# A feed-forward stage's SiLU and channel maximum: one pass per group of four channel chunks, or one pass over all 32

## The chip, the cores and the metric

The kernel runs on all 8 cores of one Trainium2 chip. The batch of 16 sequences is dealt out two to a core, every core runs the same program on its own two, and no core talks to another. The metric is the device time of the slowest core in microseconds (us). The profile shown is one execution, read on core 5, which took longest in it.

## What is computed

The reference is a transformer layer: attention with its layer norms, then a quantized feed-forward stage (BitNet style) with a depthwise convolution in it. Cut to the part that the change touches:

```python
def bit_linear(x, w):            # act_quant: per token, scale 127 / max |x| over channels
    xq = act_quant(x)            # weight_quant: to -1, 0, 1 by mean |w|
    wq = weight_quant(w)
    return einsum('bsd,hd->bsh', xq, wq)
h = bit_linear(x, w1)                                # 1024 -> 4096 channels
h = depthwise_conv1d(h, conv_w, conv_b)              # 3 taps along the tokens
h = silu(h)
return bit_linear(h, w2)                             # 4096 -> 1024 channels
```

The second `bit_linear` needs, for each token, the largest |silu(h)| over all 4096 channels before it can quantize any of them. That maximum is what the changed lines compute.

## The kernel before

Each core handles its two sequences one after the other (`_seq`), with these stages in a row: layer norm and transposes, the three projections, attention, output projection and second layer norm, weight quantization (reloaded for the second sequence), the feed-forward stage (`_p5_ffn`), and a last layer norm with the output.

In `_p5_ffn` the loop runs over 16 token tiles of 128 tokens (NT = 16), so 32 tiles in all on a core. In a tile the 4096 hidden channels lie as 32 chunks (HC = 32) of 128 channels on the 128 partitions, tokens along the free dimension; `tcv` holds the tile's hidden activations, 32 chunks by 128 tokens, bf16. A tile goes like this:

- For each chunk TensorE runs 8 matmuls (L851) into one of two small PSUM tensors, `hps0` and `hps1`. It may not write one until VectorE has emptied the chunk two before (`hevac`).
- VectorE empties it with the two dequantization scales into `hgr` (L863), 130 columns wide, since the convolution wants a token on either side.
- After every fourth chunk (`c4 == 3`), VectorE runs the convolution of that group of four in six instructions (L888 to L898) into 512 columns of `tcv`.
- Still within the group, ScalarE applies SiLU to these 512 columns in place (L901). VectorE waits for it and takes the maximum of |value| over the group's four chunks for every token (L905, a strided read: for each of 128 tokens four values that lie 128 elements apart). From the second group on that goes into a scratch column block of `f12`, and a further instruction merges it into `gmax` (L912). There are 8 groups in a tile.
- After the eighth group TensorE transposes `gmax` (L914), VectorE reduces it over the partitions' 128 rows, works out the scale, and the scale is spread over the partitions (L917 to L935).
- Then for each of 8 blocks of 512 columns, GpSimd multiplies by the scale (L949), VectorE and GpSimd round by hand in five steps (L953 to L967), and TensorE runs 8 matmuls of 512 columns with the quantized weights `w2q` (L978). VectorE takes the tile's result out of PSUM (L989) and a DMA stores it (L993).

The order of the work is the order of the program text. `em.emit` appends to one stream per engine, and an engine runs its stream in order. Every VectorE instruction waits for the one before it (semaphore `dv`, through `emit`), and a wait with `None` means everything that engine had been given by then. So the instruction that waits for ScalarE at L905 holds back everything behind it on VectorE, the next group's L863 among it:

```python
em.emit("vector", lambda e, g_=g_: e.tensor_reduce(
    gmax[:] if g_ == 0 else f12[:, 0:128], ...),
    waits=[(ac, None)])
```

Of the kernel before, what the change touches and what calls it, by code (L numbers as in the profile page):

```python
# [9 lines left out]
AF = mybir.ActivationFunctionType  # L10
ALU = mybir.AluOpType
AX = mybir.AxisListType
# [10 lines left out]
HC = DH // 128  # L23
# [71 lines left out]
def rearr(t, spec, **kw):  # L95
    return t[:].rearrange(spec, **kw)
# [171 lines left out]
def _seq(ctx, s):  # L268
    nc = ctx["nc"]
    with (  # L270
        nc.sbuf_tensor(f"s{s}_xqfm", [128, DC * S], BF16) as xqfm,
        nc.sbuf_tensor(f"s{s}_ivfm", [128, S], F32) as ivfm,
    ):
        with nc.sbuf_tensor(f"s{s}_big32", [128, DC * S], BF16) as big32:
            with (
                nc.sbuf_tensor(f"s{s}_qpk", [128, DC * S], BF16) as qpk,
                nc.sbuf_tensor(f"s{s}_kpk", [128, DC * S], BF16) as kpk,
                nc.sbuf_tensor(f"s{s}_vsb", [128, NT * VW], BF16) as vsb,
            ):
                _p1_ln1(ctx, s, big32)  # L280
                _p2_qkv(ctx, s, big32, qpk, kpk, vsb, (xqfm, [0, DC * D]))
                with (
                    nc.sbuf_tensor(f"s{s}_pt", [128, 3 * S], BF16) as pt,
                    nc.sbuf_tensor(f"s{s}_oddh", [64, S], BF16) as oddh,
                    nc.sbuf_tensor(f"s{s}_qa", [65, 2 * S], BF16) as qa,
                    nc.sbuf_tensor(f"s{s}_ka", [65, 2 * S], BF16) as ka,
                    nc.sbuf_tensor(f"s{s}_mke", [64, 65], BF16) as mke,
                ):
                    ctx["ivb16"] = xqfm
                    ctx["absq"] = oddh  # L290
                    _p3_attn(ctx, s, qpk, kpk, vsb, big32, pt, ivfm, oddh,
                             qa, ka, mke)
            _p4_proj_ln(ctx, s, big32, xqfm, ivfm)
        with (
            nc.sbuf_tensor(f"s{s}_w1q", [128, DC * DH], BF16) as w1q,
            nc.sbuf_tensor(f"s{s}_w2q", [128, HC * D], BF16) as w2q,
        ):
            _p45_wquant(ctx, s, w1q, w2q)
            _p5_ffn(ctx, s, xqfm, ivfm, w1q, w2q)
# [504 lines left out]
def _p5_ffn(ctx, s, xqfm, ivfm, w1q, w2q):  # L804
    nc, dr, sb, em = ctx["nc"], ctx["dr"], ctx["sb"], ctx["em"]
    pe, dv, ac = ctx["pe"], ctx["dv"], ctx["ac"]
    sf, sws = ctx["sf"], ctx["sws"]
    fspill = []
    with (
# [25 lines left out]
        for i in range(NT):  # L835
# [3 lines left out]
            for cc in range(HC):  # L839
                idx = i * HC + cc  # L840
                g, c4 = cc // 4, cc % 4
                ps = hps[cc % 2]
                if idx >= 2:
                    w = [(dv, hevac[idx - 2])]
                else:
                    w = [(dv, None)]
                    if ctx.get("wq_rdy"):
                        w.append((sws, ctx["wq_rdy"]))
                for dc in range(DC):
                    em.emit("tensor", lambda e, ps=ps, cc=cc, dc=dc,  # L850
                            j0=j0, j1=j1, t0=t0: e.matmul(  # L851
                        ps[:, j0:j1],
                        w1q[:, dc * DH + cc * 128:dc * DH + cc * 128 + 128],
                        xqfm[:, dc * S + t0 + j0:dc * S + t0 + j1],
                        start=(dc == 0), stop=(dc == DC - 1)),
                        inc=pe if dc == DC - 1 else None,
                        waits=w if dc == 0 else [])
                gb = (g % 2) * 520
                hw = [(pe, None)]
                if len(convd) >= 2:  # L860
                    hw.append((dv, convd[-2]))
                em.emit("vector", lambda e, ps=ps, c4=c4, gb=gb, j0=j0, j1=j1,
                        t0=t0: e.scalar_tensor_tensor(  # L863
                    hgr[:, gb + c4 * 130 + j0:gb + c4 * 130 + j1],
                    ps[:, j0:j1], sb["iwcol"][:, 0:1],
                    ivfm[:, t0 + j0:t0 + j1], ALU.mult, ALU.mult),
                    waits=hw)
                if i == 0:
                    em.emit("vector", lambda e, c4=c4, gb=gb: e.memset(
                        hgr[:, gb + c4 * 130:gb + c4 * 130 + 1], 0.0))  # L870
                if i == NT - 1:
                    em.emit("vector", lambda e, c4=c4, gb=gb: e.memset(
                        hgr[:, gb + c4 * 130 + 129:gb + c4 * 130 + 130], 0.0))
                hevac.append(dv.n)
                if c4 == 3:
                    def hv(j, gb=gb):
                        return bass.AP(hgr, gb + j, [[1040, 128], [130, 4],
                                                     [1, 128]])
                    def wmap(j, g=g):
                        return bass.AP(sb["cw"], 3 * (4 * g) + j,  # L880
                                       [[3 * HC, 128], [3, 4], [0, 128]])
                    cbm = bass.AP(sb["cb"], 4 * g,
                                  [[HC, 128], [1, 4], [0, 128]])
                    out3 = bass.AP(tcv, g * 512, [[HC * 128, 128], [128, 4],
                                                  [1, 128]])
                    tm3 = bass.AP(tmpg, 0, [[512, 128], [128, 4], [1, 128]])
                    em.emit("vector", lambda e, hv=hv, wmap=wmap, out3=out3:
                            e.tensor_tensor(out3, hv(1), wmap(1), ALU.mult))  # L888
                    em.emit("vector", lambda e, cbm=cbm, out3=out3:
                            e.tensor_tensor(out3, out3, cbm, ALU.add))  # L890
                    em.emit("vector", lambda e, hv=hv, wmap=wmap, tm3=tm3:
                            e.tensor_tensor(tm3, hv(0), wmap(0), ALU.mult))
                    em.emit("vector", lambda e, out3=out3, tm3=tm3:
                            e.tensor_tensor(out3, out3, tm3, ALU.add))
                    em.emit("vector", lambda e, hv=hv, wmap=wmap, tm3=tm3:
                            e.tensor_tensor(tm3, hv(2), wmap(2), ALU.mult))
                    em.emit("vector", lambda e, out3=out3, tm3=tm3:
                            e.tensor_tensor(out3, out3, tm3, ALU.add))  # L898
                    convd.append(dv.n)
                    g_ = cc // 4  # L900
                    em.emit("scalar", lambda e, g_=g_: e.activation(  # L901
                        tcv[:, g_ * 512:(g_ + 1) * 512],
                        tcv[:, g_ * 512:(g_ + 1) * 512], AF.Silu),
                        waits=[(dv, None)])
                    em.emit("vector", lambda e, g_=g_: e.tensor_reduce(  # L905
                        gmax[:] if g_ == 0 else f12[:, 0:128],
                        bass.AP(tcv, g_ * 512, [[HC * 128, 128], [1, 128],
                                                [128, 4]]),
                        AX.X, ALU.max, apply_absolute_value=True),
                        waits=[(ac, None)])  # L910
                    if g_ > 0:
                        em.emit("vector", lambda e: e.tensor_max(  # L912
                            gmax[:], gmax[:], f12[:, 0:128]))
            em.emit("tensor", lambda e: e.transpose(  # L914
                tmps[:], gmax[:], sb["eye32"][:]), inc=pe,
                waits=[(dv, None), (dv, None)])
# [12 lines left out]
                waits=[(dv, None)])  # L929
# [6 lines left out]
                    waits=[(pe, None)])  # L936
# [6 lines left out]
            for g in range(8):  # L943
# [3 lines left out]
                if i >= 1 and g == 0:  # L947
# [6 lines left out]
                        waits=[(ctx["gc"], yg)])  # L954
# [8 lines left out]
                    waits=[(ctx["gc"], dg)])  # L963
# [7 lines left out]
                for cc4 in range(4):  # L971
                    cc = g * 4 + cc4
# [3 lines left out]
                    for nb in range(2):  # L976
# [7 lines left out]
                            waits=w2w if (nb == 0 and cc4 == 0) else [])  # L984
# [103 lines left out]
```

How the kernel before makes its waits and increments, by code:

```python
        def play(e, fn=fn, wl=wl, inc=inc, k=k):  # L72
            for h, v in wl:
                e.wait_ge(h, v)
            ins = fn(e)
            if inc is not None and ins is not None:
                ins.then_inc(inc.h, k)
# [82 lines left out]
        @blk.sync  # L160
        def _(sync):
            sync.wait_ge(sems["so0"].h, sems["so0"].n)
            sync.wait_ge(sems["so1"].h, sems["so1"].n)
```

## Time and profile before

| | us |
|---|---|
| two timed runs | 8022.25 and 8098.92, median 8060.58 |
| the profiled execution | 8044.94 |
| span of its slowest core (core 5), first to last instruction | 8043.3 |
| spans of the eight cores | 8003.8 to 8043.3 |
| first feed-forward stage in it (window used here) | 2050 to 3970 |
| second feed-forward stage (window used here) | 5900 to 7900 |

In the rows below PE is TensorE (PEld its weight loads), DVE is VectorE, ACT is ScalarE and POOL is GpSimd. A row of a group of instructions reads: line, engine, operation, output and inputs with shapes, count, then the busy time in us and the mean ns of one, then the idle time of the engine just before them in us and what ended it. A row of the timeline reads: start in us, length in us, engine, line, operation, count, and in brackets the idle time before it and its releaser. "PEclk" is TensorE's granted clock as a share of full speed.

### The profile page before, as it was taken

Reading aid. Unit: us, or ns where it says so; the run is one execution under the profiler, and the core shown is the slowest. Engines: PE = TensorE matmul, PEld = TensorE weight load, DVE = VectorE, ACT = ScalarE, POOL = GpSimd, SP = SyncE. Lnnn points to the kernel's source line nnn. Section 1 sums busy time; section 2 is a strip of 40 time slices with the busy share of each in tenths; the row PEclk is TensorE's granted clock in tenths of the full one; section 3 lists DMA queues with packets and bytes.
Section 4 is the critical chain, followed back from the end, with each engine's and each line's share of the span. In section 5 each row is a group of like instructions: output and inputs, shape, how many; then the busy total and the mean of one; then the engine's idle time right before and its main releaser. Section 6 shows DMA issues by size and latency. Waiting matters only on the chain. (4 is left out here: it accounts for less than half of the span.)

```text
span 8043.3 us, 59576 instructions; the slowest of 8 cores (8003.8 to 8043.3 us)
## 1 busy us (share of the span) xinstructions
PE 3718.8 (46%) x17510; PEld 1781.4 (22%) x17510; DVE 4463.2 (55%) x6308; ACT 1248.6 (16%) x1418; POOL 675.0 (8%) x630
## 2 busy tenths in 40 slices
PE   0688886220334343343416888862224334344341
PEld 0322222110222222222203222221112222222221
DVE  5334444557666666666653444436546666666665
ACT  0035554000000000000000465540000000000000
POOL 0000000000011111111110000000001111111111
PEclk9877887665666666666657877776666666666665
DMA  6200001114300000000042000011020000000004
GB/s 192 52 6 6 8 8 21 37 37 141 118 3 6 3 6 6 3 6 3 6 144 58 7 7 6 8 26 37 34 86 6 6 3 6 3 6 6 3 6 128
DMA packets 59132, 251.98 MB, mean 31 GB/s; under 512 B 6720, under 2 KB 6848, under 8 KB 55232
## 3 DMA queue, kind: packets, MB, share of 16 engines
q1 hardware_dynamic: 40992, 197.32, 7.7%
q0 software_dynamic: 17824, 50.86, 2.3%
q8 instruction: 147, 2.41, 0.1%
q14 instruction: 169, 1.38, 0.1%
HBM read 185.77 MB, written 67.11 MB: 31 GB/s over the span
## 5 line engine op out<-in xcount | busy, mean ns | idle before, releaser
L851 PE MATMUL s_hps<-s_xqfm,s_w1q 128*128 128x130 bf16 (+1 forms) x8192 | 864.1, 293 | 1665.2 <-DVE s_hgr L863 1232.4
L851 PEld LDWEIGHTS s_hps<-s_xqfm,s_w1q 128*128 128x128 bf16 x8192 | 775.9, 134 | 1759.3 <-issue 1737.1
L534 ACT ACTIVATE s_pt<-s_sc 128x1024 bf16<-128x1024 f32 x1024 | 1048.7, 1024 | 691.2 <-PE s_sc L521 620.1
L978 PE MATMUL s_fp<-s_w2q,s_gq 128*128 128x512 bf16 x2048 | 707.9, 508 | 716.6 <-DVE s_gq L967 716.6
L521 PE MATMUL s_sc<-s_qa,s_ka 65*128 65x512 bf16 x2048 | 753.8, 459 | 142.7 <-ACT s_pt L534 27.3
L901 ACT ACTIVATE s_tcv<-s_tcv 128x512 bf16<-128x512 bf16 x256 | 161.1, 629 | 3777.8 <-DVE s_tcv L898 3777.8
L547 PE MATMUL s_atps<-s_pt,s_vsb 128*65 128x512 bf16 x2048 | 668.6, 423 | 0.0
L961 DVE SCALAR_TENSOR_TENSOR s_f<-s_db,s_r 128x512 f32<-128x512 f32 x256 | 396.1, 1547 | 406.6 <-POOL s_db L958 406.6
L949 POOL TENSOR_TENSOR s_yb<-s_tcv,s_sgb 128x512 f32<-128x512 bf16 x256 | 296.1, 1157 | 3780.5 <-DVE s_sgb L935 3748.4
L863 DVE SCALAR_TENSOR_TENSOR s_hgr<-s_hps,iwcol,s_ivfm 128x130 bf16<-128x130 f32 (+1 forms) x1024 | 361.3, 353 | 437.0 <-PE s_hps L851 376.7
L978 PEld LDWEIGHTS s_fp<-s_w2q,s_gq 128*128 128x128 bf16 x2048 | 225.2, 118 | 1188.5 <-issue 1102.8
L556 DVE COPY s_ivfm<-s_atps 65x2048 f32<-65x2048 f32 x32 | 73.2, 2287 | 674.7 <-PE s_atps L547 674.7
L564 DVE RECIPROCAL s_ivfm<-s_ivfm 1x2048 f32<-1x2048 f32 x32 | 414.2, 12944 | 3.3
L958 POOL TENSOR_TENSOR s_db<-s_yb,s_r 128x512 f32<-128x512 f32 x256 | 323.1, 1262 | 614.6 <-DVE s_r L955 614.6
L905 DVE TENSOR_REDUCE s_f<-s_tcv 128x128 f32<-128x512 bf16 x224 | 227.2, 1014 | 213.9 <-ACT s_tcv L901 213.9
L521 PEld LDWEIGHTS s_sc<-s_qa,s_ka 65*128 65x128 bf16 x2048 | 163.8, 105 | 700.1 <-issue 687.6
L547 PEld LDWEIGHTS s_atps<-s_pt,s_vsb 128*65 128x65 bf16 x2048 | 252.3, 124 | 298.7 <-issue 126.3
L725 PE MATMUL s_trp<-eye16s,s_xqt 128*128 128x128 bf16 x256 | 32.4, 306 | 603.1 <-DVE s_xqt L262 603.1
L378 PE MATMUL s_qps<-s_big,s_xqfm 128*128 128x512 bf16 x1024 | 249.0, 412 | 39.2 <-DMA s_xqfm<-wq_t 39.2
L246 ACT ACTIVATE sdc<-st 128x1 f32<-128x1 f32 x128 | 26.0, 203 | 1160.0 <-DVE st L241 1159.9
L579 PE MATMUL s_sc<-s_ivfm,ones 1*64 1x512 f32 x256 | 169.5, 818 | 76.3 <-DVE s_xqfm L566 48.4
L676 PE MATMUL s_op<-s_wo,s_big 128*128 128x512 bf16 x512 | 174.3, 516 | 40.3 <-DMA s_wo<-wo_t 40.3
(123 smaller groups left out, 3723.1 us busy)
## 6 DMA issues: line engine op xcount, KB each, us to landing
s_xint<-x SPq DMA_DIRECT2D x64, 512.0 KB, 3.9
p0st<-w_t SPq DMA_DIRECT2D x8, 2048.0 KB, 8.9
p0st<-w_t SPq DMA_DIRECT2D x32, 512.0 KB, 3.3
x2scr<-s_x2t SPq DMA_DIRECT2D x32, 512.0 KB, 2.9
s_wst<-w_t SPq DMA_DIRECT2D x16, 1024.0 KB, 5.0
s_wst<-w_t SPq DMA_DIRECT2D x32, 512.0 KB, 3.2
fscr<-s_ft POOLq DMA_DIRECT2D x32, 512.0 KB, 3.0
s_frl<-fscr SPq DMA_DIRECT2D x32, 512.0 KB, 6.5
```

Of the source, the lines that this page charges most:

```text
L378: wo=wofs[wb]: e.matmul(ps[:, nb * 512:(nb + 1) * 512], wtens[:, wo + dc * D + oc * 128:wo + dc * D + oc * 128 + 128], xn1[:, dc * S + nb ...
L521: em.emit("tensor", lambda e, kt=kt, nb=nb, b=b, j=j: e.matmul(scp[j][:, nb * 512:(nb + 1) * 512], ka[:, b * S + kt * 128:b * S + kt * 128 ...
L534: em.emit("scalar", lambda e, p=p, j=j: e.activation(pt[:, p * S + j * Q:p * S + (j + 1) * Q], scp[j][:], AF.Exp), waits=w)
L547: em.emit("tensor", lambda e, kt=kt, nb=nb, h=h, p=p, j=j: e.matmul(atps[0:65, j * Q + nb * 512:j * Q + (nb + 1) * 512], vsb[:, kt * VW + ...
L564: em.emit("vector", lambda e: e.reciprocal(ivr[64:65, :], ivr[64:65, :]))
L851: j0=j0, j1=j1, t0=t0: e.matmul(ps[:, j0:j1], w1q[:, dc * DH + cc * 128:dc * DH + cc * 128 + 128], xqfm[:, dc * S + t0 + j0:dc * S + t0 + j1],
L863: t0=t0: e.scalar_tensor_tensor(hgr[:, gb + c4 * 130 + j0:gb + c4 * 130 + j1], ps[:, j0:j1], sb["iwcol"][:, 0:1], ivfm[:, t0 + j0:t0 + j1] ...
L905: em.emit("vector", lambda e, g_=g_: e.tensor_reduce(gmax[:] if g_ == 0 else f12[:, 0:128], bass.AP(tcv, g_ * 512, [[HC * 128, 128], [1, 128],
L949: em.emit("gpsimd", lambda e, ts=ts: e.tensor_tensor(rearr_ap3(yb), rearr_ap3(ts), sgv, ALU.mult), inc=ctx["gc"], waits=yw)
L958: em.emit("gpsimd", lambda e: e.tensor_sub(db2[:], yb[:], r02[:]), inc=ctx["gc"], waits=[(dv, r0d)])
L961: em.emit("vector", lambda e: e.scalar_tensor_tensor(f12[:], db2[:], 1.5, r02[:], ALU.is_gt, ALU.add), waits=[(ctx["gc"], dg)])
L978: gq4=gq4, cc4=cc4: e.matmul(ps[:, nb * 512:(nb + 1) * 512], gq4[:, cc4 * 128:(cc4 + 1) * 128], w2q[:, cc * D + nb * 512:cc * D + (nb + 1) ...
```

## The change

The SiLU and the maximum are taken out of the group's branch and out of the loop over chunks. They are issued once per tile, after the last chunk: one ScalarE instruction over all 4096 columns of `tcv`, in place, and one VectorE reduction that reads, for each of 128 tokens, 32 values 128 elements apart, straight into `gmax`. The merging instruction is gone. The reduction still waits for ScalarE, and the transpose behind it (now L905) still waits for the reduction.

```diff
                     convd.append(dv.n)
-                    g_ = cc // 4
-                    em.emit("scalar", lambda e, g_=g_: e.activation(
-                        tcv[:, g_ * 512:(g_ + 1) * 512],
-                        tcv[:, g_ * 512:(g_ + 1) * 512], AF.Silu),
-                        waits=[(dv, None)])
-                    em.emit("vector", lambda e, g_=g_: e.tensor_reduce(
-                        gmax[:] if g_ == 0 else f12[:, 0:128],
-                        bass.AP(tcv, g_ * 512, [[HC * 128, 128], [1, 128],
-                                                [128, 4]]),
-                        AX.X, ALU.max, apply_absolute_value=True),
-                        waits=[(ac, None)])
-                    if g_ > 0:
-                        em.emit("vector", lambda e: e.tensor_max(
-                            gmax[:], gmax[:], f12[:, 0:128]))
+            em.emit("scalar", lambda e: e.activation(tcv[:], tcv[:], AF.Silu),
+                    waits=[(dv, None)])
+            em.emit("vector", lambda e: e.tensor_reduce(
+                gmax[:], rearr(tcv, "p (c t) -> p t c", c=HC), AX.X, ALU.max,
+                apply_absolute_value=True), waits=[(ac, None)])
```

On VectorE, at the border between two groups in the middle of a tile, before (L863 is the emptying of the next group's four chunks, L888 its convolution's first instruction):

```order
L896 TENSOR_TENSOR s_tmpg<-s_hgr,cw_sb 128x512
L898 TENSOR_TENSOR s_tcv<-s_tcv,s_tmpg 128x512
L905 TENSOR_REDUCE s_f<-s_tcv 128x128
L912 TENSOR_TENSOR s_gmax<-s_gmax,s_f 128x128
L863 SCALAR_TENSOR_TENSOR s_hgr<-s_hps,iwcol,s_ivfm 128x130 x4
L888 TENSOR_TENSOR s_tcv<-s_hgr,cw_sb 128x512
```

The same border on VectorE after the change:

```order
L896 TENSOR_TENSOR s_tmpg<-s_hgr,cw_sb 128x512
L898 TENSOR_TENSOR s_tcv<-s_tcv,s_tmpg 128x512
L863 SCALAR_TENSOR_TENSOR s_hgr<-s_hps,iwcol,s_ivfm 128x130 x4
L888 TENSOR_TENSOR s_tcv<-s_hgr,cw_sb 128x512
L890 TENSOR_TENSOR s_tcv<-s_tcv,cb_sb 128x512
```

The reduction and the merge have left the border, and the emptying of the next chunks stands right behind the convolution.

On VectorE at the end of a tile, before (L917 reads the transposed `gmax`):

```order
L898 TENSOR_TENSOR s_tcv<-s_tcv,s_tmpg 128x512
L905 TENSOR_REDUCE s_f<-s_tcv 128x128
L912 TENSOR_TENSOR s_gmax<-s_gmax,s_f 128x128
L917 TENSOR_REDUCE sdc<-s_tmp 128x1
L919 TENSOR_SCALAR sdc<-sdc 128x1
```

The same place after the change, where lines behind the diff have moved up by nine:

```order
L898 TENSOR_TENSOR s_tcv<-s_tcv,s_tmpg 128x512
L902 TENSOR_REDUCE s_gmax<-s_tcv 128x128
L908 TENSOR_REDUCE sdc<-s_tmp 128x1
L910 TENSOR_SCALAR sdc<-sdc 128x1
L912 RECIPROCAL sdc<-sdc 128x1
```

One reduction (L902) now stands there in place of a reduction and a merge, and it is the only one of the tile.

On ScalarE one sequence's feed-forward stage holds, in the piece of the difference below, 128 instructions before and 16 after:

```order
-L901 ACTIVATE s_tcv<-s_tcv 128x512 x128
+L900 ACTIVATE s_tcv<-s_tcv 128x4096 x16
```

The work per element is the same; the number of instructions falls to an eighth. On TensorE and GpSimd no instruction is moved.

## Rows read from the trace of the kernel before

**Rows 1.** The page's first part: busy time of each engine over the span.

```profile
PE 3718.8 (46%) x17510; PEld 1781.4 (22%) x17510; DVE 4463.2 (55%) x6308; ACT 1248.6 (16%) x1418; POOL 675.0 (8%) x630
```

**Rows 2.** The page's fourth part, the chain that ended last, by engine.

```profile
DMA 1%; DVE 0%; issue 0%; ACT 0%; DVEq 0%; POOLq 0%; ACTq 0%; SPq 0%
```

**Rows 3.** Busy time of each engine in the two feed-forward stages.

```profile
core 5: us, PE busy (x) PEld busy (x) DVE busy (x) ACT busy (x) POOL busy (x), PEclk, DMA share, GB/s
2050.00:3970.00 1920.00, 766.20 (x4932) 487.44 (x4933) 1181.56 (x2084) 77.42 (x122) 299.27 (x255) 0.65 0.04 13
5900.00:7900.00 2000.00, 785.07 (x5120) 504.70 (x5120) 1227.33 (x2194) 81.82 (x129) 302.81 (x258) 0.65 0.02 6
```

**Rows 4.** Timeline of one group in the middle of a tile, 2582 to 2595 us.

```profile
2582.05 0.42 DVE L898 TENSOR_TENSOR s_tcv<-s_tcv,s_tmpg 128x512 bf16<-128x512 bf16 x1
2582.63 0.63 ACT L901 ACTIVATE s_tcv<-s_tcv 128x512 bf16<-128x512 bf16 x1 [8.60 <-DVE s_tcv L898]
2583.43 1.01 DVE L905 TENSOR_REDUCE s_f<-s_tcv 128x128 f32<-128x512 bf16 x1 [0.95 <-ACT s_tcv L901]
2584.55 0.29 DVE L912 TENSOR_TENSOR s_gmax<-s_gmax,s_f 128x128 f32<-128x128 f32 x1
2584.94 0.81 DVE L863 SCALAR_TENSOR_TENSOR s_hgr<-s_hps,iwcol,s_ivfm 128x130 bf16<-128x130 f32 x2
...
2585.44 3.62 PE L851 MATMUL s_hps<-s_xqfm,s_w1q 128*128 128x130 bf16 x32 [6.00 <-DVE s_hgr L863]
2586.64 0.35 DVE L863 SCALAR_TENSOR_TENSOR s_hgr<-s_hps,iwcol,s_ivfm 128x130 bf16<-128x130 f32 x1 [0.89 <-PE s_hps L851]
2587.51 0.35 DVE L863 SCALAR_TENSOR_TENSOR s_hgr<-s_hps,iwcol,s_ivfm 128x130 bf16<-128x130 f32 x1 [0.51 <-PE s_hps L851]
...
2594.56 0.81 DVE L863 SCALAR_TENSOR_TENSOR s_hgr<-s_hps,iwcol,s_ivfm 128x130 bf16<-128x130 f32 x2
```

**Rows 5.** Groups of instructions by line and shape: SiLU, maximum and merge.

```profile
L905 DVE TENSOR_REDUCE s_f<-s_tcv 128x128 f32<-128x512 bf16 x224 | 227.2, 1014 | 213.9 <-ACT s_tcv L901 213.9
...
L901 ACT ACTIVATE s_tcv<-s_tcv 128x512 bf16<-128x512 bf16 x256 | 161.1, 629 | 3777.8 <-DVE s_tcv L898 3777.8
...
L912 DVE TENSOR_TENSOR s_gmax<-s_gmax,s_f 128x128 f32<-128x128 f32 x224 | 65.5, 293 | 23.6 <-DVE s_f L905 0.5
...
L905 DVE TENSOR_REDUCE s_gmax<-s_tcv 128x128 f32<-128x512 bf16 x32 | 32.5, 1014 | 33.2 <-ACT s_tcv L901 33.2
```

**Rows 6.** Groups by line and shape: other ScalarE functions and in-order reductions elsewhere.

```profile
L534 ACT ACTIVATE s_pt<-s_sc 128x1024 bf16<-128x1024 f32 x1024 | 1048.7, 1024 | 691.2 <-PE s_sc L521 620.1 <-PE s_atps L547 4.7
...
L203 DVE TENSOR_REDUCE t1c<-p0st 128x1 f32<-128x1024 f32 x32 | 39.0, 1220 | 35.4 <-DMA p0st<-w_t 35.3
...
L203 DVE TENSOR_REDUCE t1c<-p0st 128x1 f32<-128x4096 f32 x8 | 35.4, 4420 | 34.7 <-DMA p0st<-w_t 34.7
...
L246 ACT ACTIVATE sdc<-st 128x1 f32<-128x1 f32 x128 | 26.0, 203 | 1160.0 <-DVE st L241 1159.9
```

**Rows 7.** Timeline: first-stage matmuls at a tile's start, second-stage bursts near its end.

```profile
2567.38 1.10 PE L851 MATMUL s_hps<-s_xqfm,s_w1q 128*128 128x130 bf16 x16 [1.26 <-DVE s_hgr L863]
2568.19 0.82 DVE L863 SCALAR_TENSOR_TENSOR s_hgr<-s_hps,iwcol,s_ivfm 128x130 bf16<-128x130 f32 x2 [0.49 <-PE s_hps L851]
...
2664.34 1.89 PE L978 MATMUL s_fp<-s_w2q,s_gq 128*128 128x512 bf16 x8 [1.92 <-DVE s_gq L967]
...
2669.45 3.20 PE L978 MATMUL s_fp<-s_w2q,s_gq 128*128 128x512 bf16 x8 [3.23 <-DVE s_gq L967]
```

**Rows 8.** Granted clock (third number from the end) in four stretches of a tile.

```profile
2566.90:2575.30 8.40, 2.21 (x32) 1.91 (x32) 6.02 (x11) 0.63 (x1) 0.59 (x1) 0.87 0.15 62
2575.30:2584.90 9.60, 3.62 (x32) 3.30 (x32) 6.33 (x12) 0.63 (x1) 0.00 (x0) 0.68 0.01 3
2584.90:2594.50 9.60, 3.62 (x32) 3.29 (x32) 6.33 (x12) 0.63 (x1) 0.00 (x0) 0.50 0.00 0
...
2668.00:2676.00 8.00, 4.63 (x15) 1.73 (x16) 5.28 (x8) 0.00 (x0) 2.79 (x3) 0.79 0.00 1
```

## The prediction

> **What bounds the kernel now.** I read the page's first part first. VectorE is the busiest engine, at 55% of the span, TensorE stands at 46% and ScalarE at 16% [rows 1]. No engine is near full, so the time is made of engines waiting for one another, and shares of the whole span don't say where. The chain that ended last gives no help: it explains only about 1% [rows 2], since it stops soon at waits that it can't follow. So I went to the stage that the change touches. The two feed-forward stages have VectorE busy for 1181.56 of 1920 us and for 1227.33 of 2000 us, some 61%, against 77.42 and 81.82 us on ScalarE [rows 3].
>
> Then the timeline of one group. VectorE is where to look, because its stream is never ahead of anything. The convolution's last instruction ends at 2582.05 + 0.42 = 2582.47. ScalarE runs its SiLU for 0.63, and VectorE stands idle for 0.95 meanwhile. Then come the maximum (1.01) and the merge (0.29), and only at 2584.94 does VectorE empty the next chunk. TensorE had waited for exactly that, 6.00 us [rows 4]. A group lasts 2594.56 - 2584.94 = 9.62 us, in which TensorE works for 3.62. VectorE's instructions and its waits, end to end, are the length of the stage. In the 9.62 us it also waits for TensorE, 0.89 and 0.51, while the third and the fourth chunk are made.
>
> **What the change takes off VectorE.** The groups give it for all 256 groups: the maximum 227.2 + 32.5 busy with 213.9 + 33.2 idle ahead of it, the merge 65.5 with 23.6 ahead [rows 5]. Together that is 595.9 us, all of it on the path. The timeline agrees: 2584.94 - 2582.47 = 2.47 for a group, of which the 0.10 between any two VectorE instructions (from 2584.84 to 2584.94) stays, so 2.37 go; a tile's first group has no merge and loses 0.39 less. 224 x 2.37 + 32 x 1.98 is 594.
>
> **Is another engine late next?** TensorE's burst for a group starts at 2585.44 and ends at 2589.06, 4.12 us after VectorE began emptying [rows 4]. It includes the first two chunks of the following group. VectorE now comes for these after 9.62 us and will come after 9.62 - 2.37 = 7.25 us. TensorE has 3.1 us to spare, so the border's saving is not given back there, and it costs nothing elsewhere: GpSimd, the DMAs and the PSUM tensors keep their order. If this cover were gone (a burst over 7.25 us), TensorE would set the group's length, but that needs twice its present time.
>
> **What it adds.** After a tile's last convolution, ScalarE passes over 4096 columns, VectorE over as many, and TensorE's transpose waits for both. Behind the waiting reduction on VectorE stands the chain to the scale, and behind that the whole quantization; the other engines' streams wait for it. Nothing hides these two instructions. There are 32 such places.
>
> - Handover. A SiLU of 629 ns costs VectorE 213.9 / 224 = 0.955 of idleness [rows 5], so 0.33 goes to the two signals. 0.33 stays, once a tile.
> - SiLU over 4096 columns. One element takes 203 ns [rows 6] and 512 take 629 [rows 5]: 0.834 ns an element, so 203 + 4095 x 0.834 = 3.62 us. From below, the slope between 512 and the 1024 columns of the attention's 1024 ns [rows 6] is 0.771, which gives 3.39. From above, eight times 629 ns is 5.03. I take 3.62, as it is the same kind of operand.
> - The maximum over 4096 columns, the term that matters most. No row shows it. In-order reductions take 1220 ns for 1024 elements and 4420 for 4096 [rows 6], so 1.042 ns an element and 153 ns to start. By that 512 elements would be 686 ns; the group's maximum takes 1014 [rows 5], 328 more. Either each of its 512 reads is slower, because the next value lies 128 elements on, or each of its 128 output columns costs something. By the first the new one takes 153 + 8 x (1014 - 153) = 7.04 us, by the second 4420 + 328 = 4.75. The bounds are 4.42 (in order, one output) and 8 x 1014 = 8.11. I take 7.04: the nearest row is the same operation with the same stride, scaled by its elements.
> - The table load. 33.2 less 32 x 0.955 leaves 2.6 us in the removed idle time: ScalarE loads its table at the first SiLU of each sequence. This stays, so 2.6 comes back.
>
> The reduction's surplus can be set beside a rule. The Trainium skill (SBUF — State Buffer, Specifications (TRN2), the row on cachelines) says that reads which each cross to a new 16-byte line pay a penalty, whatever their order. Here every read does so, and the surplus of 328 ns for 512 reads in rows 5 and 6 agrees with it; whether it is the reads or the columns that pay, no row here shows. By that rule the penalty grows with the reads, and the sum is the one of 7.04; without it, the one of 4.75.
>
> **The sum.** Added: 32 x (0.33 + 3.62 + 7.04) = 351.7, and 2.6 makes 354.3. Removed: 595.9. Net 241.6 us less. The profiled execution took 8044.94, so 8044.9 - 241.6 = 7803 us. (Its span was 8043.3; the 1.6 around it stay.) The median of the timed runs is 8060.58, 16 higher, of two runs 77 us apart; I leave the sum on the profiled execution. With the lower bounds (3.39 and 4.42) the added part is 263.1 and the time 7712; with the upper (5.03 and 8.11) it is 433.6 and the time 7883.
>
> **Rival 1: the surplus belongs to the output columns.** Then the maximum takes 4.75, the added part is 32 x 8.70 + 2.6 = 281, the saving 315 and the time 7730. For it: the 328 ns divide over 128 columns as easily as over 512 reads, and a reduction has to close a result at each. Against it: nothing but the stride being large. This is nearly as likely as the forecast.
>
> **Rival 2: TensorE's clock stays up.** With VectorE's pause gone, TensorE idles for 7.25 - 3.62 = 3.63 us between bursts where it idled for 6.00 [rows 4]. Now the groups run at a granted clock of 0.50 to 0.68, and at a tile's start, right after the second stage's matmuls, at 0.87 [rows 8]. There VectorE waited 0.49 for the third and fourth chunk together [rows 7] where it waits 0.89 + 0.51 = 1.40 at the lower level of 1.2 GHz. If all 256 groups ran so, 256 x 0.91 = 233 us more would go: 7570. Against it: in the second stage a burst of 1.89 us at 2664.34 is followed by an idle time of 3.23 us, and the burst behind it takes 3.20 again [rows 7], with the clock at 0.79 over that stretch [rows 8]. So idling about as long as 3.63 us lets the clock fall. The Trainium skill (TensorE: Matmul & The Clock Gate, Part 1) has it that activity releases the throttle and idleness brings it back, with an advice to keep gaps short; the rows just cited agree with the direction, and by the rule taken alone the time would be this rival's. I expect a few us of this at most.
>
> **Rival 3, the slower side: the long strided pass.** It works at one place, L902, 32 times. The change breaks even where SiLU, handover and maximum reach (595.9 - 2.6) / 32 = 18.54 us a tile, so where the maximum takes 14.6; it is over 2% slower (161 us, 5.0 a tile) from 19.6. That would need 4.8 ns a read against 1.68 now. If every read cost what a whole column of four costs now, 1014 / 128 = 7.9 ns, the maximum would be 32.4 us and the time 8045 - 595.9 + 32 x 36.4 + 2.6 = 8616. For it only that the reads of a column now reach over 8 KB of a partition instead of 1 KB. Against it: the group's row shows no such price with the same stride.
>
> **Rival 4: within 2%.** The saving must fall below 161 us, so SiLU and maximum together must pass 13.2 us, which is the sum of both upper bounds. Or TensorE takes part of it back; its 3.1 us of slack speak against this.
>
> **How the numbers follow.** Forecast 0.51 (7803), rival 1 0.38 (7730), rival 2, whole or in good part, 0.04, rival 4 0.06, rival 3 0.01. A measurement of this kernel can tell about 2% from no change. The first three cases are all faster by more than that: 0.93 faster, 0.06 same, 0.01 slower. The range takes in rival 1 less half the spread of the runs before (39 us), 7690, and on the other side the forecast with that spread and some of the upper bound of the SiLU, 7855.
>
> **What would show it.** Right: VectorE goes from L898 to L863 in 0.1 us; a group lasts some 7.25 us; TensorE's idle time before the burst is near 3.6; L900 takes 3.62 us x32 and L902 7.0 x32; the feed-forward stages are shorter by 120 us each, and no other stage has moved. The length of L902 alone decides between the forecast and rivals 1 and 3. Wrong: a VectorE wait for TensorE ahead of the first chunk of a group, waits at L863 for the third and fourth chunk well below 1.40 us a group (rival 2), or a stage elsewhere that changes by more than a few us.

## The result, and the profile after

The changed kernel takes 7813.17 us (median of 11 runs) where the kernel before takes 8033.81 (10 runs): a ratio of 0.9693, with a 95% interval from 0.9655 to 0.973 (the two medians alone would give 0.9725). On the profiled execution before (8044.94) the ratio is 7798 us, from 7767 to 7828 by its interval; the sum had given 7803. One execution of the changed kernel (7877.94), in which the cores of one die had a lower granted clock than the others, is left out of the ratio, and the single executions of two experiments below (the reads in memory order, the ten reductions), in which the same is seen, are compared by the cores of the other die alone. The profiled execution of the changed kernel took 7776.41, with a span of 7774.8 on its slowest core, core 3.

The first part of the page (core 3), the counterpart of [rows 1]:

```profile
PE 3683.3 (47%) x17510; PEld 1767.4 (23%) x17510; DVE 4361.9 (56%) x5860; ACT 1203.2 (15%) x1194; POOL 675.1 (9%) x630
```

VectorE has lost 448 instructions but only 101 us of work, while the kernel lost more than twice that. So more than half of what went was waiting. VectorE's share has risen by one point, and the page says nothing more than that.

The timeline of one group in the middle of a tile (core 3), the counterpart of [rows 4]:

```profile
2536.36 0.42 DVE L898 TENSOR_TENSOR s_tcv<-s_tcv,s_tmpg 128x512 bf16<-128x512 bf16 x1
2536.88 0.81 DVE L863 SCALAR_TENSOR_TENSOR s_hgr<-s_hps,iwcol,s_ivfm 128x130 bf16<-128x130 f32 x2
2537.38 3.62 PE L851 MATMUL s_hps<-s_xqfm,s_w1q 128*128 128x130 bf16 x32 [3.64 <-DVE s_hgr L863]
2538.59 0.35 DVE L863 SCALAR_TENSOR_TENSOR s_hgr<-s_hps,iwcol,s_ivfm 128x130 bf16<-128x130 f32 x1 [0.89 <-PE s_hps L851]
2539.45 0.35 DVE L863 SCALAR_TENSOR_TENSOR s_hgr<-s_hps,iwcol,s_ivfm 128x130 bf16<-128x130 f32 x1 [0.51 <-PE s_hps L851]
...
2544.15 0.81 DVE L863 SCALAR_TENSOR_TENSOR s_hgr<-s_hps,iwcol,s_ivfm 128x130 bf16<-128x130 f32 x2
```

VectorE goes from L898 to L863 in 0.1 us. The group lasts 2544.15 - 2536.88 = 7.27 us, where it lasted 9.62. TensorE's burst is as long as before and its idle time has shrunk from 6.00 to 3.64. The waits for the third and fourth chunk are the same 0.89 and 0.51. Nothing has moved in under the saving.

The timeline of the same tile's end:

```profile
2571.99 0.42 DVE L898 TENSOR_TENSOR s_tcv<-s_tcv,s_tmpg 128x512 bf16<-128x512 bf16 x1
2572.57 3.62 ACT L900 ACTIVATE s_tcv<-s_tcv 128x4096 bf16<-128x4096 bf16 x1 [113.74 <-DVE s_tcv L898]
2576.35 6.99 DVE L902 TENSOR_REDUCE s_gmax<-s_tcv 128x128 f32<-128x4096 bf16 x1 [3.94 <-ACT s_tcv L900]
2583.48 0.45 PE L905 MATMUL s_tmp<-eye32s,s_gmax 128*128 128x128 f32 x1 [15.84 <-DVE s_gmax L902]
```

For 11 us only one engine works at a time, first ScalarE, then VectorE. This is what the change pays, 32 times. The groups by line and shape, the counterpart of [rows 5], hold its whole price:

```profile
L902 DVE TENSOR_REDUCE s_gmax<-s_tcv 128x128 f32<-128x4096 bf16 x32 | 223.6, 6986 | 129.1 <-ACT s_tcv L900 129.1
...
L900 ACT ACTIVATE s_tcv<-s_tcv 128x4096 bf16<-128x4096 bf16 x32 | 115.7, 3616 | 3446.7 <-DVE s_tcv L898 3446.7
```

That is 223.6 + 129.1 = 352.7 us on VectorE's stream, for the 595.9 that left it.

Where in the program did the time go? The two stages can be cut out by their first L863 and their last store. Core 5, before, each feed-forward stage (line, count, shortest, median and longest length in ns, then start of the first and of the last; the shapes behind that are not needed here):

```profile
L993 POOL DMA_DIRECT2D fscr<-s_ft x16: 595/595/627, 2189.8 to 4087.0; - x16
L993 POOL DMA_DIRECT2D fscr<-s_ft x16: 595/595/627, 6042.3 to 7940.3; - x16
L863 DVE SCALAR_TENSOR_TENSOR s_hgr<-s_hps,iwcol,s_ivfm x512: 351/353/356, 2054.9 to 4029.8; 128x130 bf16<-128x130 f32 x149, 128x129 bf16<-128x129 f32 x22
L863 DVE SCALAR_TENSOR_TENSOR s_hgr<-s_hps,iwcol,s_ivfm x512: 350/353/357, 5909.9 to 7882.8; 128x130 bf16<-128x130 f32 x149, 128x129 bf16<-128x129 f32 x22
```

The same on core 5 after the change:

```profile
L984 POOL DMA_DIRECT2D fscr<-s_ft x16: 595/595/627, 2164.3 to 3940.7; - x16
L984 POOL DMA_DIRECT2D fscr<-s_ft x16: 595/596/624, 5889.1 to 7671.5; - x16
L863 DVE SCALAR_TENSOR_TENSOR s_hgr<-s_hps,iwcol,s_ivfm x512: 350/353/358, 2038.3 to 3873.3; 128x130 bf16<-128x130 f32 x149, 128x129 bf16<-128x129 f32 x22
L863 DVE SCALAR_TENSOR_TENSOR s_hgr<-s_hps,iwcol,s_ivfm x512: 350/353/358, 5764.8 to 7605.4; 128x130 bf16<-128x130 f32 x149, 128x129 bf16<-128x129 f32 x22
```

The first stage went from 4087.0 - 2054.9 = 2032.1 to 1902.4 us, the second from 2030.4 to 1906.7: 129.7 and 123.7, together 253.4. Between the stages it is 1822.9 and 1824.1, and behind the last store 103.0 in both, so the rest of the program is as it was. Core 5's first stage also began 16.6 us earlier. No instruction ahead of it was changed; that part differs from core to core (before, the first stage begins between 2020.3 and 2054.9, latest on core 5), and it is most of why the profiled execution lies 22 us under the ratio's 7798. The cut also shows that the windows in the table ahead of the prediction are too short: the first stage runs to 4087, not 3970, and the second to 7940, not 7900.

### The profile page after: what moved, and what is told of

Its sections match the earlier page's. It is cut to its first block and busy times, and to the rows that moved or that the text cites. A ratio compares the mean times of both kernels' runs of the same rounds, so it can differ in the third digit from the quotient of the medians.

```text
span 7774.8 us, 57784 instructions; the slowest of 8 cores (7741.0 to 7774.8 us)
## 1 busy us (share of the span) xinstructions
PE 3683.3 (47%) x17510; PEld 1767.4 (23%) x17510; DVE 4361.9 (56%) x5860; ACT 1203.2 (15%) x1194; POOL 675.1 (9%) x630
## 3 DMA queue, kind: packets, MB, share of 16 engines
q14 instruction: 156, 1.28, 0.1%
## 5 line engine op out<-in xcount | busy, mean ns | idle before, releaser
L534 ACT ACTIVATE s_pt<-s_sc 128x1024 bf16<-128x1024 f32 x1024 | 1048.7, 1024 | 699.8 <-PE s_sc L521 628.1
L900 ACT ACTIVATE s_tcv<-s_tcv 128x4096 bf16<-128x4096 bf16 x32 | 115.7, 3616 | 3446.7 <-DVE s_tcv L898 3446.7
L863 DVE SCALAR_TENSOR_TENSOR s_hgr<-s_hps,iwcol,s_ivfm 128x130 bf16<-128x130 f32 (+1 forms) x1024 | 361.5, 353 | 425.9 <-PE s_hps L851 365.3
L902 DVE TENSOR_REDUCE s_gmax<-s_tcv 128x128 f32<-128x4096 bf16 x32 | 223.6, 6986 | 129.1 <-ACT s_tcv L900 129.1
L905 PE MATMUL s_tmp<-eye32s,s_gmax 128*128 128x128 f32 x32 | 14.3, 447 | 511.3 <-DVE s_gmax L902 511.3
L378 PE MATMUL s_qps<-s_big,s_xqfm 128*128 128x512 bf16 x1024 | 225.5, 384 | 38.6 <-DMA s_xqfm<-wq_t 38.6
```

The lines of the kernel that those rows point to most:

```text
L378: wo=wofs[wb]: e.matmul(ps[:, nb * 512:(nb + 1) * 512], wtens[:, wo + dc * D + oc * 128:wo + dc * D + oc * 128 + 128], xn1[:, dc * S + nb ...
L534: em.emit("scalar", lambda e, p=p, j=j: e.activation(pt[:, p * S + j * Q:p * S + (j + 1) * Q], scp[j][:], AF.Exp), waits=w)
L863: t0=t0: e.scalar_tensor_tensor(hgr[:, gb + c4 * 130 + j0:gb + c4 * 130 + j1], ps[:, j0:j1], sb["iwcol"][:, 0:1], ivfm[:, t0 + j0:t0 + j1] ...
L902: em.emit("vector", lambda e: e.tensor_reduce(gmax[:], rearr(tcv, "p (c t) -> p t c", c=HC), AX.X, ALU.max, apply_absolute_value=True), wa ...
```

## The experiments

Experiments measured together share their runs of the kernel before. Lines are those of each kernel, so the same statement can have another number.

One measure serves for all of them: the two feed-forward stages, cut out on every core as above (from the first emptying of a chunk to the start of the last store) and added up. It is sharper than the time of the whole kernel. Before, the cores differ by 34.6 us in when the first stage begins and by 35.3 in what lies between the stages, but only by 3.8 in the two stages themselves.

| kernel | two stages, mean of eight cores, us | shortest and longest core |
|---|---|---|
| before | 4063.0 | 4061.6 to 4065.4 |
| changed | 3812.7 | 3804.7 to 3820.2 |
| SiLU in the group, maximum once | 3711.7 | 3707.6 to 3717.9 |
| maximum one group later | 3863.8 | 3856.4 to 3870.8 |
| reads in memory order | 3731.3 | 3727.0 to 3736.5 |
| ten reductions | 3932.4 | 3926.5 to 3937.6 |
| maximum twice | 4036.1 | 4029.1 to 4041.2 |
| maximum by halves | 3597.9 | 3593.0 to 3600.4 |
| TensorE kept busy | 3623.0 | 3620.6 to 3625.7 |
| the last two together | 3511.2 | 3509.4 to 3512.4 |

### SiLU back in the group, the maximum once: what counts is VectorE's stream

```diff
                     convd.append(dv.n)
+                    g_ = cc // 4
+                    em.emit("scalar", lambda e, g_=g_: e.activation(
+                        tcv[:, g_ * 512:(g_ + 1) * 512],
+                        tcv[:, g_ * 512:(g_ + 1) * 512], AF.Silu),
+                        waits=[(dv, None)])
-            em.emit("scalar", lambda e: e.activation(tcv[:], tcv[:], AF.Silu),
-                    waits=[(dv, None)])
```

> The SiLU goes back into the group (512 columns each), the maximum stays one pass at the tile's end. My theory: what counts is only what stands on VectorE's stream. ScalarE's seven earlier SiLUs run beside VectorE's next group; at the tile's end 0.955 us of waiting is left where the change has 3.62 + 0.4 = 4.03. So 32 x 3.0 = 98 us less than the changed kernel and about 339 less than before: ratio to before 0.958. Rival (it was the number of signals and ScalarE's split work that cost): the SiLU back in the group brings the time back up, 0.97 or more.

Measured: 7705.45 us, ratio 0.9594 (0.9559 to 0.9628). The groups by line and shape of this kernel (core 5):

```profile
L905 DVE TENSOR_REDUCE s_gmax<-s_tcv 128x128 f32<-128x4096 bf16 x32 | 223.6, 6986 | 30.7 <-ACT s_tcv L901 30.7
L901 ACT ACTIVATE s_tcv<-s_tcv 128x512 bf16<-128x512 bf16 x256 | 161.6, 631 | 3420.1 <-DVE s_tcv L898 3420.1
```

ScalarE has eight times as many instructions again, and 46 us more work than in the changed kernel. Yet the kernel is faster, since VectorE waits 30.7 us for it where it waited 129.1. That wait is 98 us shorter, as expected, and the ratio is the expected 0.958 within its interval. Against the changed kernel the two stages are 101 us shorter; the two ratios, from different series, say 80 with some 41 of uncertainty. Splitting the SiLU cost the kernel nothing that shows here; waiting for it did.

### The maximum one group later: the wait apart from the work

The function holds the old maximum and merge. It is called behind the next group's fourth emptying and at the tile's end:

```diff
+            def flush_max():
+                while pend_max:
+                    g_, an = pend_max.pop(0)
...
                 hevac.append(dv.n)
                 if c4 == 3:
+                    flush_max()
...
-                    em.emit("vector", lambda e, g_=g_: e.tensor_reduce(
...
+                    pend_max.append((g_, ac.n))
+            flush_max()
```

> The kernel before, but a group's maximum and merge are issued one group later, behind the next group's four emptyings; only the last group's stands at the tile's end. No operation is left out. My theory: the waits for ScalarE (213.9 + 33.2 us, less the last group's 32 x 0.955 and about what the table load costs) go, 214 us, and the busy time of maximum and merge stays: about 7831, ratio 0.973. So the pause without work would be as much of the old cost as all that the change brought net. Rival (VectorE's pause was TensorE's time anyway, and the emptying waits longer for TensorE now): ratio 0.985 to 1.0, with waits at L863 above 376 us in all.

Measured: 7823.72 us, ratio 0.9753 (0.9715 to 0.9791). The groups of this kernel (core 4), and its wait for TensorE at the emptying (us in total, times, longest):

```profile
L844 DVE TENSOR_REDUCE s_f<-s_tcv 128x128 f32<-128x512 bf16 x224 | 229.5, 1025 | 50.4 <-ACT s_tcv L917 30.3 <-DVE s_hgr L878 0.7
...
L844 DVE TENSOR_REDUCE s_gmax<-s_tcv 128x128 f32<-128x512 bf16 x32 | 32.9, 1028 | 3.4 <-DVE s_hgr L878 0.2
...
DVE s_hgr L878 <- PE s_hps L866: 375.7, 480, 53.3
```

The idle time ahead of the maximum fell from 247.1 us [rows 5] to 53.8, that is by 193, and the ratio stands for 198 (give or take 31), the two stages for 199. My 214 had left out the 0.1 us that lies between any two VectorE instructions, which now stands ahead of the maxima that no longer wait. The rival is out: it wanted waits for TensorE above 376 us and a ratio of 0.985 or more, and the waits at the emptying are 375.7 us where the same core had 375.3 before. So TensorE's work had not been hiding the pause. With every operation still there, this reordering alone gives four fifths of what the change gives (199 of 250 us in the two stages).

### Reads in memory order: is it the reads or the columns?

```diff
-                gmax[:], rearr(tcv, "p (c t) -> p t c", c=HC), AX.X, ALU.max,
+                gmax[:], rearr(tcv, "p (t c) -> p t c", c=HC), AX.X, ALU.max,
```

> The changed kernel with the maximum's 4096 reads in memory order (each output column takes 32 neighbouring values, so the maximum is over the wrong values; counts and columns are the same). Reads theory (each strided read is dear): the maximum falls from 6.99 to about 4.4 us and the time by 82 us, waits unchanged. Columns theory (the 128 outputs or their closing are dear): it stays above 4.7, up to 7.0, and the time hardly moves.

The group by line and shape:

```profile
L902 DVE TENSOR_REDUCE s_gmax<-s_tcv 128x128 f32<-128x4096 bf16 x32 | 141.4, 4420 | 129.1 <-ACT s_tcv L900 129.1
```

With the same 128 output columns the reduction takes 4420 ns, to the nanosecond what the in-order reduction of 4096 elements (of f32) into a single value takes [rows 6]. The columns are free; the strided reads cost. In the one execution of this kernel (7743.33 us) the median of cores 0 to 3 is 7684.3 us, against 7768.0 in the changed kernel's profiled execution. That is 84, and the two stages are 81 shorter, with 32 x (6.986 - 4.420) = 82 expected.

### Ten reductions side by side: from which distance?

Behind the maximum, in tile 1 of each sequence, ten reductions of this form follow:

```diff
+            if i == 1:
+                em.emit("vector", lambda e: e.tensor_reduce(
+                    f12[:, 0:128], bass.AP(tcv, 0, [[HC * 128, 128], [32, 128], [1, 32]]), AX.X,
+                    ALU.max, apply_absolute_value=True))
...
```

> The changed kernel with ten more reductions after the maximum in one tile of each sequence, into scratch; all read 4096 bf16 values. Eight have 128 output columns of 32 values at a distance of 1 (in order), 2, 4, 8, 16, 32, 64, 128 elements (neighbouring columns one element apart); one has 16 columns of 256 values 16 apart; one 512 columns of 8 in order. Reads theory with the rule on 16-byte lines: 4.4 us up to a distance of 4 elements (8 bytes), 7.0 from 8 elements (16 bytes) on, the same for 16 columns; 4.4 for 512 columns in order. Rival: the length grows step by step with the distance. Rival: it goes by the number of columns, so 512 columns cost more than 128 and 16 columns less. Total time about 115 us above the changed kernel.

The instructions that write the scratch (core 5; in order of the lines: in order, then distances of 2, 4, 8, 16, 32, 64 and 128 elements, then 16 columns at a distance of 16, then 512 columns in order):

```profile
L906 DVE TENSOR_REDUCE s_f<-s_tcv x2: 4419/4420/4420, 2229.6 to 6010.3; 128x128 f32<-128x4096 bf16 x2
L909 DVE TENSOR_REDUCE s_f<-s_tcv x2: 4419/4419/4419, 2234.2 to 6014.8; 128x128 f32<-128x4096 bf16 x2
L912 DVE TENSOR_REDUCE s_f<-s_tcv x2: 4419/4420/4420, 2238.7 to 6019.3; 128x128 f32<-128x4096 bf16 x2
L915 DVE TENSOR_REDUCE s_f<-s_tcv x2: 7329/7329/7329, 2243.2 to 6023.8; 128x128 f32<-128x4096 bf16 x2
L918 DVE TENSOR_REDUCE s_f<-s_tcv x2: 7466/7466/7467, 2250.6 to 6031.3; 128x128 f32<-128x4096 bf16 x2
L921 DVE TENSOR_REDUCE s_f<-s_tcv x2: 6981/6981/6981, 2258.2 to 6038.8; 128x128 f32<-128x4096 bf16 x2
L924 DVE TENSOR_REDUCE s_f<-s_tcv x2: 6984/6986/6989, 2265.3 to 6045.9; 128x128 f32<-128x4096 bf16 x2
L927 DVE TENSOR_REDUCE s_f<-s_tcv x2: 6984/6984/6985, 2272.4 to 6053.0; 128x128 f32<-128x4096 bf16 x2
L930 DVE TENSOR_REDUCE s_f<-s_tcv x2: 7467/7467/7467, 2279.5 to 6060.1; 128x16 f32<-128x4096 bf16 x2
L933 DVE TENSOR_REDUCE s_f<-s_tcv x2: 4419/4419/4419, 2287.0 to 6067.7; 128x512 f32<-128x4096 bf16 x2
```

There is one step, between 4 and 8 elements, that is between 8 and 16 bytes. Distances in between were not tried. Up to 8 bytes a distance costs nothing, from 16 bytes on 4096 reads cost 2.6 to 3.0 us more, and going on to 256 bytes adds nothing. The distances of 8 and 16 elements are a little dearer still (7.33 and 7.47), which no theory of mine had. 512 columns cost as much as one.

This step is where the Trainium skill (SBUF — State Buffer, Specifications (TRN2)) puts it: its lines have 16 bytes, and at least two reads of each are wanted. At a distance of 8 bytes the rows give two reads a line and full speed, at 16 bytes one read a line and the penalty.

The ten add (4.42 x 4 + 7.33 + 7.47 x 2 + 6.98 x 3) x 2 + 20 x 0.1, or 124 us, and 115 was expected. In the one execution (7990.16 us) the median of cores 4 to 7 is 7887.1 us against 7760.7 in the changed kernel, 126 more, and the two stages are 120 longer.

### The maximum twice: is the tile's end bare?

```diff
                 apply_absolute_value=True), waits=[(ac, None)])
+            em.emit("vector", lambda e: e.tensor_reduce(
+                f12[:, 0:128], rearr(tcv, "p (c t) -> p t c", c=HC), AX.X, ALU.max,
+                apply_absolute_value=True), waits=[])
```

> The changed kernel with the maximum at the tile's end done twice, the second time into scratch. If the tile's end has no cover, as the prediction's sum takes it: 32 x (6.99 + 0.10) = 227 us more, all of it in the two feed-forward stages. Rival (TensorE or GpSimd would have been late there anyway): less than 150 us more.

Measured in one execution: 8002.27 us, against 7776.41 in the changed kernel's profiled execution, 226 more. That is the fastest execution of the changed kernel, and others took up to 64 us longer, so the stages say it better: together they are 223 us longer. The groups:

```profile
L902 DVE TENSOR_REDUCE s_gmax<-s_tcv 128x128 f32<-128x4096 bf16 x32 | 223.5, 6985 | 128.8 <-ACT s_tcv L900 128.8
L905 DVE TENSOR_REDUCE s_f<-s_tcv 128x128 f32<-128x4096 bf16 x32 | 223.5, 6985 | 3.3
```

Of the 32 x (6.985 + 0.10) = 227 us of VectorE put in at that place, 223 show in the stages, on the mean of the eight cores (from 216 to 235 core by core). The tile's end is bare.

### The maximum by halves

```diff
-            em.emit("vector", lambda e: e.tensor_reduce(
-                gmax[:], rearr(tcv, "p (c t) -> p t c", c=HC), AX.X, ALU.max,
-                apply_absolute_value=True), waits=[(ac, None)])
+            em.emit("vector", lambda e: e.tensor_max(
+                mt, tcv[:, 0:2048], tcv[:, 2048:4096]),
+                waits=[(ac, None)])
+            em.emit("vector", lambda e: e.tensor_max(
+                mt[:, 0:1024], mt[:, 0:1024], mt[:, 1024:2048]))
...
+            em.emit("vector", lambda e: e.tensor_max(
+                gmax[:], mt[:, 0:128], mt[:, 128:256]))
```

> SiLU in the group as in e1_silu_group, and the maximum as five element-wise maxima over halves (2048, 1024, 512, 256, 128 columns, bf16, neighbouring elements, the last into f32). It leaves out the absolute value: the largest SiLU is taken, which is the same wherever one of a token's 4096 values passes 0.28. My theory: such an operation over 512 columns takes 425 ns (the convolution's add), so 1225, 692, 425, 292 and 292 ns with 0.1 between them, 3.3 us for 7.0: 32 x 3.66 = 117 us less than e1_silu_group, ratio to before 0.945. Rival (the halves fall to one column per cycle, 2.29 us for the first): nothing won, 0.957.

Measured: 7560.6 us, ratio 0.9407 (0.9383 to 0.9432). The groups of the five steps:

```profile
L906 DVE TENSOR_TENSOR s_gq<-s_tcv 128x2048 bf16<-128x2048 bf16 x32 | 39.2, 1226 | 30.4 <-ACT s_tcv L902 30.4
L909 DVE TENSOR_TENSOR s_gq<-s_gq 128x1024 bf16<-128x1024 bf16 x32 | 22.2, 692 | 3.3
...
L911 DVE TENSOR_TENSOR s_gq<-s_gq 128x512 bf16<-128x512 bf16 x32 | 13.6, 425 | 3.7 <-DVE s_gq L909 0.5
L913 DVE TENSOR_TENSOR s_gq<-s_gq 128x256 bf16<-128x256 bf16 x32 | 9.4, 292 | 3.3
L915 DVE TENSOR_TENSOR s_gmax<-s_gq 128x128 f32<-128x128 bf16 x32 | 9.3, 292 | 3.3
```

Five instructions with 4.0 thousand columns between them take 93.7 us and 13.6 of gaps, 107 in all, where one reduction took 223.6. From 1024 to 2048 columns the time grows by 534 ns, 0.52 a column, where the reduction takes 1.04 for a read in order, and no read is strided. By these rows 116 us should go, and 117 was expected. The two stages are 114 us shorter than with the SiLU alone in the group. The ratios say 0.9594 - 0.9407 = 0.0187 of 8034, 150 us, with some 34 of uncertainty and from two series; rows and stages are the better measure. For tokens with no SiLU value above 0.28 the largest magnitude can be missed, so this is a finding on cost and not a ready replacement.

### TensorE kept busy: the prediction's rival 2, by force

```diff
+                if c4 == 1 and cc > 1:
+                    for q in range(24):
+                        em.emit("tensor", lambda e, q=q: e.matmul(
+                            tmps[:], w1q[:, q * 128:(q + 1) * 128],
+                            xqfm[:, 0:128], start=True, stop=True))
```

> e1_silu_group with 24 further matmuls of 128 columns, whose results nobody reads, on TensorE behind the second chunk of every group but a tile's first; there TensorE has 3.1 us to spare and they take 24 x 107 ns = 2.6 at the lower clock level. Clock theory (the prediction's rival 2): kept busy, TensorE is granted the higher level and the waits for the third and fourth chunk fall from 1.40 to 0.49 us a group: up to 224 x 0.91 = 204 us less than e1_silu_group, ratio to before about 0.935. Its own rival (the clock does not rise, or the extra work makes the emptying wait): 0.96 or more.

The edit stands on the kernel with the SiLU in the group. Measured: 7596.91 us, ratio 0.9453 (0.9431 to 0.9475). By the ratios that is 113 us (give or take 33) less than with the SiLU alone in the group; by the two stages it is 89. For comparison, three groups of the changed kernel's timeline, by windows (TensorE's granted clock is the third number from the end):

```profile
2536.90:2544.20 7.30, 3.62 (x32) 3.29 (x32) 5.06 (x11) 0.00 (x0) 0.00 (x0) 0.50 0.00 0
2544.20:2551.40 7.20, 3.62 (x32) 3.29 (x32) 4.98 (x10) 0.00 (x0) 0.00 (x0) 0.50 0.00 0
2551.40:2558.70 7.30, 3.63 (x32) 3.29 (x32) 5.05 (x11) 0.00 (x0) 0.00 (x0) 0.67 0.01 2
```

And three groups of this kernel (core 2):

```profile
2502.50:2509.70 7.20, 3.55 (x56) 3.26 (x56) 5.59 (x12) 0.63 (x1) 0.00 (x0) 1.00 0.00 0
2509.70:2516.20 6.50, 3.55 (x56) 3.26 (x56) 5.03 (x10) 0.63 (x1) 0.00 (x0) 0.99 0.01 3
2516.20:2523.50 7.30, 4.61 (x56) 4.36 (x56) 5.04 (x11) 0.63 (x1) 0.00 (x0) 0.78 0.00 0
```

In the first two of them TensorE works off 56 matmuls in the time that 32 took, at the full 2.4 GHz, and a group that runs so lasts 6.5 us. Over the whole first stage of this core the granted clock is 0.77, against 0.66 on the same core with the SiLU alone in the group. What VectorE still waits (groups by line and shape; the first is that of all tiles but a sequence's first and last):

```profile
L868 DVE SCALAR_TENSOR_TENSOR s_hgr<-s_hps,iwcol,s_ivfm 128x130 bf16<-128x130 f32 x896 | 316.3, 353 | 235.7 <-PE s_hps L851 165.3 <-DVE s_hgr L868 3.5 <-DVE s_tcv L903 0.9
...
L988 DVE TENSOR_SCALAR s_ft<-s_fp,sdc,iwcol 128x1024 f32<-128x1024 f32 x32 | 43.0, 1344 | 111.4 <-PE s_fp L977 111.4
```

With the SiLU alone in the group, core 2 had 281.2 us of such waits at the emptying, and 334.4 idle in all against 235.7. At the tile's output it had 88.9 us against 111.4, so some of the gain is given back there; why was not tried. The gain is real, but of the 204 us that were possible a good two fifths came (89). The third window above shows one reason: its granted clock is 0.78, and in its burst VectorE waits 0.89 and 0.51 us again for the third and fourth chunk, as at the lower level.

### The last two together

> e6_tree and e7_busy_pe together. If both gains are on VectorE's stream they add up: ratio to before about 0.92. If they hide each other, no better than the better of the two.

The edit is the sum of the two. Measured: 7497.9 us, ratio 0.9328 (0.9307 to 0.935), the fastest of all, though not the 0.92 expected. It leaves out the absolute value, as its first part does. VectorE's wait at the emptying with the halves alone, and with both (each on core 1):

```profile
L864 DVE SCALAR_TENSOR_TENSOR s_hgr<-s_hps,iwcol,s_ivfm 128x130 bf16<-128x130 f32 x896 | 316.1, 353 | 335.0 <-PE s_hps L852 282.1 <-DVE s_hgr L864 1.5 <-DVE s_tcv L899 0.9
...
L869 DVE SCALAR_TENSOR_TENSOR s_hgr<-s_hps,iwcol,s_ivfm 128x130 bf16<-128x130 f32 x896 | 316.1, 353 | 248.2 <-PE s_hps L852 181.0 <-DVE s_hgr L869 2.0 <-DVE s_tcv L904 0.9
```

By the ratios the second gain is 63 us behind the halves where it was 113 without them, each with some 30 of uncertainty, which would leave open whether the two add up. The stages settle it: kept busy, TensorE takes 89 us off the kernel with the SiLU in the group and 87 off the kernel with the halves. The two gains alone are 114 and 89, together 203, and both edits at once took off 201. They add up, and the 0.92 was too much because the second gain had been priced at 204.

## Why the prediction was right

**VectorE's stream is the stage.** It rested on the timeline of one group. Every kernel here agrees: taking idle time off it (the deferred maximum, the SiLU in the group), adding work to it (the maximum twice) and making its work cheaper (the reads in order, the halves) each moved the two stages by what the rows of VectorE said, to some 6 us.

**Removed: 595.9 us.** The border is gone as read; a group lasts 7.27 us for the 7.25 worked out. TensorE kept its 3.1 us of slack (its burst ends at 2541.00, VectorE comes back at 2544.15).

**Added: 354.3 us.** It is 352.7. The SiLU was put at 3.62 and takes 3.616. The table loads stayed, two of 1.28 us. The handover, (129.1 - 2.6) / 32 - 3.616, is 0.34 for 0.33.

**The maximum over 4096 columns: 7.04.** It takes 6.986. This was the choice that carried the forecast against rival 1, and it had been close (0.51 against 0.38): nothing in the rows of before told a strided read from an output column, so that the right one was taken is in part luck. Rival 1 wanted 4.75 and fell: reads in order into 128 columns take 4.42, into 512 columns 4.42. The 328 ns of surplus belonged to the reads. Its size had the small error that the surplus was scaled from 512 reads: (6986 - 1014) / 3584 is 1.666 ns a read, for 1.682 in the sum.

**Rival 2** was put at "a few us at most", and less waiting for TensorE did come, a few us of it. On core 5 VectorE waited for TensorE before (line waiting, line waited for, us in total, times, longest):

```profile
DVE s_hgr L863 <- PE s_hps L851: 376.7, 481, 52.0
DVE s_ft L989 <- PE s_fp L978: 87.1, 31, 4.0
DVE s_ft L989 <- PE s_hps L851: 4.3, 1, 4.3
```

and after:

```profile
DVE s_hgr L863 <- PE s_hps L851: 357.9, 481, 46.4
DVE s_ft L980 <- PE s_fp L969: 94.0, 31, 4.0
DVE s_ft L980 <- PE s_hps L851: 2.6, 1, 2.6
```

The waits at the emptying fell by 18.8 and those at the tile's output rose from 91.4 to 96.6, 13.6 less in all. Core 5 is not the rule: added up in the same way, the eight cores lie between 21.3 less (core 4) and 3.4 more (core 1), with a mean of 7.4 less. With 241.6 + 1.7 (for the maximum) + 7.4, the sum is 250.7 where the two stages show 250.3 on the mean of the eight cores. Whether the 7.4 come from the clock is not shown: in core 5's two stages it is granted 0.65 and 0.65 before, 0.65 and 0.66 after. Kept busy by force, TensorE is granted more and the waits do fall, so the mechanism is real. The change hardly sets it off: in the three groups shown above, each with an idle time of some 3.6 us ahead of TensorE's burst, the clock is granted at 0.50, 0.50 and 0.67.

**Rivals 3 and 4** had nothing to them. Strided reads over 8 KB cost what they cost over 1 KB (1.67 ns a read beyond the first 512, and 1.68 within them), and no engine was late.

**The time.** 7803 was built on one execution; by that execution and the measured ratio it would be 7798. That the two lie within 5 us is luck, as the interval is some 30 us wide to either side. What the cuts of the stages bear out is the sum itself, 241.6 for 250.3.

## What to carry to other kernels

Where one engine's in-order stream paces a stage, look at what it waits for in the middle of its own work. The change batched two operations and won 3.1%. On VectorE's stream that is 102 us of work less (325.2 before, 223.6 after) and 142 of idle time less (270.7 and 129.1). Taking the wait away without batching anything already won 2.5%, and leaving the SiLU with ScalarE in small pieces, with the one consumer late, won 4.1%. Before batching a producer, ask whether its pieces ran beside the bottleneck.

A strided reduction should be priced by where its reads fall and not by its outputs, and a single execution with a few variants side by side settles such a price better than any argument.

## What the runs showed of the hardware that was not expected

- VectorE's reduction of 4096 bf16 values takes 4.42 us up to a distance of 8 bytes, as much as the f32 rows in order [rows 6], which give 1.04 ns a read. At 256 bytes it is 1.67 ns a read (6986 ns for 4096 reads, 1014 for 512). At 16 and 32 bytes it is dearest, 7.33 and 7.47 us for 4096 reads against 6.98 to 6.99. Why those two stand out is open. The number of output columns (1, 128, 512) does not change the 4.42 us.
- 24 matmuls a group that nobody reads shorten the two stages by 89 us (87 with the halves), with the granted clock in core 2's first stage at 0.77 where it was 0.66.
- The group's maximum takes 1025 to 1028 ns on average when it stands behind the emptying, and 1014 where it stood alone behind the SiLU's wait. In the deferred kernel TensorE works beside it (on core 4, 1.03 us at 2566.08 beside a burst, 1.01 at 2574.87 behind the end of a shorter one); what lengthens it was not tried.
